# GpSimd makes m and the turn fractions of sub-tiles two to four, and TensorE spreads the three maxima over partitions

## The reference, cut to what matters

```python
# x: (32, 128, 64, 2), real and imaginary part of C; H = 128 states, N = 64, L = 1024
A   = -exp(inv_A_real) + 1j * A_imag;  dtA = A * exp(log_dt)
Cc  = B * C * (exp(dtA) - 1) / A
h   = 2 * einsum('chn,hnl->chl', Cc, exp(dtA * ell)).real       # (32, 128, 1024)
h   = h + layernorm(h) @ attn_w.T + attn_b
y   = layernorm(h)
out = h + y @ W.T + b + sum_e softmax(y @ Wr.T)[e] * 2 * (y @ A[e].T) @ Bm[e].T
```

## Time and profile before

| | |
|---|---|
| median of 3 runs | 817.31 us (816.65 to 817.73) |
| the profiled execution's own time | 814.75 us |
| its span, first to last instruction | 812.9 us, so 1.85 us lie around it |
| PE busy | 776.4 us, 96% |
| DVE busy | 626.1 us, 77% |
| ACT busy | 527.2 us, 65% |
| POOL busy | 6.2 us, 1%, in 21 instructions |
| mean granted TensorE clock | 0.989 of full speed |

### The profile page before, as it was taken

One profiled execution on the slowest core, in us unless ns is written; L12 is line 12 of the kernel. 1 busy time (PEld: TensorE's weight loads), 2 busy tenths in 40 slices (PEclk: granted clock), 3 DMA queues, 4 the chain that ended last, 5 costly groups with the idle time before them and its releaser, 6 DMA issues.

```text
span 812.9 us, 14991 instructions
## 1 busy us (share of the span) xinstructions
PE 776.4 (96%) x5390; PEld 390.0 (48%) x5390; DVE 626.1 (77%) x1250; ACT 527.2 (65%) x884; POOL 6.2 (1%) x21
## 2 busy tenths in 40 slices
PE   3777899999999999999999999999999999999998
PEld 2643344444444444444444444444444444444443
DVE  6799797778777877787778777777887787778522
ACT  5777785767677666757677576667767575765210
POOL 2000000000000000000000000000000000000000
PEclk9989999999999999999999999999999999999999
DMA  8839543435333233334333333433324243423223
GB/s 298 280 72 166 107 98 66 91 59 98 77 76 72 64 85 67 82 77 94 63 73 74 71 83 66 97 77 68 81 55 93 60 89 77 90 52 74 56 52 77
DMA packets 185709, 72.28 MB, mean 89 GB/s; under 512 B 174097, under 2 KB 179089, under 8 KB 185561
## 3 DMA queue, kind: packets, MB, share of 16 engines
q1 hardware_dynamic: 185592, 71.90, 40.2%
q10 hardware_dynamic: 96, 0.13, 0.0%
HBM read 14.06 MB, written 16.78 MB: 38 GB/s over the span
## 4 chain that ended last, share of the span: by engine, by line
PE 88%; DVE 6%; issue 3%; ACT 2%; DMA 0%; SPq 0%; POOL 0%; POOLq 0%; DVEq 0%; ACTq 0%
PE ps_g L549 39%; PE ps_g L489 39%; PE ps_a L480 5%; PE ps_g L560 2%; PE ps_g L681 1%; PE ps_p L537 1%; DVE stage L1287 1%; DVE params L994 1%; PE ps_p L539 1%; DVE wa_lo L1279 0%; PE ps_p L554 0%; ACT decay L728 0%; DVE h_tok L1149 0%; DVE h_tok L1188 0%; DVE result L1287 0%
## 5 line engine op out<-in xcount | busy, mean ns | idle before, releaser
L489 PE MATMUL ps_g<-wa_hi,x 128*128 128x512 f16 x1024 | 270.1, 379 | 2.6 <-DMA x<-x_tok 1.6
L549 PE MATMUL ps_g<-wf_hi,x 128*128 128x512 f16 x992 | 265.2, 380 | 0.6 <-DVE h_tok L1188 0.6
L489 PEld LDWEIGHTS ps_g<-wa_hi,x 128*128 128x128 f16 x1024 | 97.6, 98 | 122.8 <-issue 6.6
L489 PE MATMUL ps_g<-wa_lo,x 128*128 128x512 f16 x512 | 153.6, 379 | 0.0
L549 PE MATMUL ps_g<-wf_lo,x 128*128 128x512 f16 x496 | 149.3, 380 | 0.0
L549 PEld LDWEIGHTS ps_g<-wf_hi,x 128*128 128x128 f16 x992 | 95.0, 98 | 107.5 <-issue 2.2
L1250 DVE SCALAR_TENSOR_TENSOR result<-ps_g,unscale,h_tok 128x1024 f32<-128x1024 f32 x31 | 39.8, 1284 | 84.2 <-PE ps_g L560 84.2
L752 ACT ACTIVATE junk<-ps_a,stat 128x1024 bf16<-128x1024 f32 x32 | 35.6, 1114 | 76.9 <-DVE stat L1152 76.8
L489 PEld LDWEIGHTS ps_g<-wa_lo,x 128*128 128x128 f16 x512 | 50.1, 98 | 60.1
L549 PEld LDWEIGHTS ps_g<-wf_lo,x 128*128 128x128 f16 x496 | 48.5, 98 | 58.5 <-issue 0.5
L758 ACT ACTIVATE junk<-h_tok,stat 128x1024 bf16<-128x1024 f32 x32 | 36.7, 1148 | 59.1 <-DVE stat L1192 59.1
(11 more groups left out here) (208 smaller groups left out, 919.3 us busy)
## 6 DMA issues: line engine op xcount, KB each, us to landing
out<-result SPq DMA_DIRECT2D x124, 128.0 KB, 2.1
stage<-in_L_ffn_W SPq DMA_DIRECT2D x8, 512.0 KB, 13.8
x_raw<-in_x SPq DMA_DIRECT2D x38, 64.0 KB
wf_hi<-in_x SPq DMA_DIRECT2D x1, 2048.0 KB, 9.8
h_tok<-in_L_attn_weight SPq DMA_DIRECT2D x2, 512.0 KB, 3.9
x<-in_L_attn_weight SPq DMA_DIRECT2D x2, 512.0 KB, 6.9
result<-in_L_attn_weight SPq DMA_DIRECT2D x2, 512.0 KB, 8.8
x<-x_tok SPq DMA_TRANSPOSE x64, 3.2
```

The source lines that it names most:

```text
L489: mm = pe.matmul(ps[:, o, :], x1_part(part, ps is ps_g2)[:, k, :], ws[:, k, o * HALF:(o + 1) * HALF], start=k == 0 and part == 0 and ws is ...
L549: pe.matmul(ps_g2[:, o, :], xs[:, k, :], ws[:, k, o * HALF:(o + 1) * HALF], start=k == 0 and xs is x2_hi and ws is wf_hi, stop=False)
```

## The change

`partition_all_reduce` is gone from GpSimd. For each bound TensorE now transposes the column of 128 values into one row of PSUM, DVE takes the maximum of the row, and TensorE multiplies that one value by a row of 128 ones, which puts it on every partition. GpSimd takes over the subtraction of `round_turns` and the three instructions of `make_m` for sub-tiles (0, 1), (1, 0) and (1, 1); from (2, 0) on all stays on DVE. GpSimd's small products for the factor k are written in another order, with `wexp` last, and ACT's wait for it goes from `s_pre_pool` 4 to 10.

```diff
+BY_POOL = (1, 2, 3)
@@ tensor
+            def turn_m_tops():
+                pe.wait_ge(s_x_squares, 1)
+                pe.wait_ge(s_pre_dve, EXPS + 26)
+                for k in range(2):
+                    mm = pe.transpose(ps_a[0:1, 1, k * P:(k + 1) * P], m_top[:, k:k + 1], ident[:, :])
+                mm.then_inc(s_tops_t, 1)
+            def spread_m_top():
+                pe.wait_ge(s_row_top, 2)
+                pe.matmul(spread(ps_a[:, 1, :]), ones_row[:, :], top_row[:, 2:3]).then_inc(s_wall, 1)
+            def turn_weight_tops(k):
+                pe.wait_ge(s_top, k + 1)
+                pe.transpose((ps_x, ps_p)[k][0:1, P:2 * P], top[:, k:k + 1], ident[:, :]).then_inc(s_tops_t, 1)
+            def spread_weight_top(k):
+                pe.wait_ge(s_row_top, k + 3)
+                pe.matmul(spread((ps_x, ps_p)[k][:, :]), ones_row[:, :], top_row[:, 3:4]).then_inc(s_wall, 1)
@@
                 mm.then_inc(s_pre_pe, 1)
+            turn_m_tops()
+            spread_m_top()
             square_attn(5, 8)
@@
             s4(0, 0)
+            turn_weight_tops(0)
             square_ffn(10, 11)
+            spread_weight_top(0)
@@
             turn_weight(4)
-            pe.wait_ge(s_top, 2)
+            turn_weight_tops(1)
+            spread_weight_top(1)
+            pe.wait_ge(s_power, 6)
             turn_weight(5)
@@ gpsimd
+            pool.wait_ge(s_small, 64)
+            (den, k_re, k_im, then after s_pre_dve EXPS: k1, ga, ga, den, k_re, k_im, wexp)
-            (the three partition_all_reduce)
+            def fractions(T, i):
+                pool.wait_ge(s_round, 2 * T + i + 1)
+                pool.tensor_tensor(turn[:, :, :], turn[:, :, :], phase[:, :, :], ALU.subtract).then_inc(s_frac, 1)
+            fractions(0, 1)
+            make_m(0, 1)
+            fractions(1, 0)
+            make_m(1, 0)
+            fractions(1, 1)
+            make_m(1, 1)
@@ vector
+            m_row_top()
             scale_m(0, 3)
@@
             weight_norms(0, ps_g2[:, 0, 0:P])
+            weight_row_top(0)
@@
             weight_norms(1, ps_p[:, 0:P])
+            weight_row_top(1)
             split_scales(1)
             attn_lo(4)
-            make_m(0, 1)
             make_u(0, 1)
```

More of the change, by code:

```diff
@@ L963, in _, with make_m @@
                                steps_a[:, 2:NA].unsqueeze(2).broadcast_to((P, KA, N)), ALU.mult).then_inc(s_pre_pool, 1)
[L964 to L983, removed]
+            def make_m(T, i):
+                J = 2 * T + i
+                pool.wait_ge(s_xt_sb, T + 1)
+                pool.wait_ge(s_s4, J)
+                pool.wait_ge(s_m, J)
+                pool.wait_ge(s_q, 2)
+                for part, dst in enumerate((m, m_im)):
+                    c, f = m_factors(T, i, part)
+                    pool.tensor_tensor(dst[:, :, :].rearrange("p h (a c) -> p h a c", a=KA), c, f, ALU.mult)\
+                        .then_inc(s_terms, 1)
+                pool.wait_ge(s_terms, 2 * J + 2)
+                pool.tensor_tensor(m[:, :, :], m[:, :, :], m_im[:, :, :], ALU.add).then_inc(s_m, 1)
+            def fractions(T, i):
[7 more added lines that the diff above has]
+            make_m(1, 1)
         @block.vector
@@ L1014, in _ @@
[L1014 to L1020, removed]
@@ L1027, in _ @@
[L1027 to L1033, removed]
@@ L1311, in split_lora_b @@
                                   ALU.subtract).then_inc(s_lbn, 1)
+            for tile, value in ((ones[:, :], 1.0), (ones_row[:, :], 1.0), (half_pi[:, :], pi / 2), (quarter[0:N, :], 0.25),
+                                (quarter[N:P, :], 0.0), (eps[:, :], EPS), (steps_a[:, 0:1], 0.5),
+                                (steps_a[:, 1:2], 1.0)):
+                last = dve.memset(tile, value)
+            last.then_inc(s_fill, 1)
+            dve.wait_ge(s_fill, 1)
+            dve.wait_ge(s_small, 64)
@@ new lines, in _ @@
+            link(dve.tensor_scalar, exp_out, exp_in, 1 / factorial(7), None, ALU.mult)
+            for k in range(6, 0, -1):
+                link(dve.scalar_tensor_tensor, out=exp_out, in0=exp_out, scalar=1 / factorial(k), in1=exp_in,
+                                              op0=ALU.add, op1=ALU.mult)
+            link(dve.tensor_scalar, exp_k.bitcast(U32), exp_k, 127.0, 2.0 ** 23, ALU.add, ALU.mult)
+            link(dve.scalar_tensor_tensor, out=exp_out, in0=exp_out, scalar=1.0, in1=exp_k, op0=ALU.add,
+                                          op1=ALU.mult)
@@ new lines, in _ @@
+            assert done[0] == EXPS + 26
+            for dst, part in ((wa, 0), (wb, 1)):
+                tt(dst.rearrange("p s a n -> p (s a) n"), w2.rearrange("p s a n -> p (s a) n"),
+                   g[:, part:part + 1, :].broadcast_to((P, 2 * KA, N)), ALU.mult)
+            tt(qn[:, :, 0:N], wa[:, 0, :, :], wb[:, 1, :, :], ALU.subtract)
+            link(dve.scalar_tensor_tensor, out=qn[:, :, N:2 * N], in0=wa[:, 1, :, :], scalar=-1.0,
+                                          in1=wb[:, 0, :, :], op0=ALU.mult, op1=ALU.subtract)
@@ L1314, in _ @@
+            tt(qn[:, :, 2 * N:3 * N], wb[:, 1, :, :], wa[:, 0, :, :], ALU.subtract)
+            assert done[0] == PRE
+            m_row_top()
             scale_m(0, 3)
@@ L1366, in _ @@
             ffn_lo(15)
-            make_m(1, 0)
             dve.wait_ge(s_wf_0, 32)
```

167 lines of the change are left out of this document (93 added, 74 removed).

## The result

| | before | after |
|---|---|---|
| time, median of 6 runs each on one chip | 817.05 us (814.50 to 818.19) | 821.67 us (820.22 to 825.95) |
| after / before | | 1.0067, 95% interval 1.0047 to 1.0087 |
| profiled execution: time, span | 814.75, 812.9 us | 821.36, 819.5 us |
| start of `s4(1, 1)` in it | 100.36 us | 105.27 us |

The change made the kernel slower. The forecast was 821.7 us with a chance of 0.7 for slower, and both hold. The two profiled executions are 6.6 us apart, more than the 5.5 us of the ratio, and the two medians are 4.6 apart.

A forecast was written before the change was run, and what follows sets the result against it. PE, busy 709.0 of 712.5 us from s4(1, 1) on, was taken as the bound, so prologue delays count. They build to a start 4.4 later: 817.31 + 4.4 = 821.7 us, range 817.4 to 823.6.

The forecast's parts named there:

- The frame: From s4(1, 1) on, instructions are the same and PE is busy, so the end moves by what its start moves.
- The last stretch: Rounding to s4(1, 1): GpSimd's fractions and m alternate with DVE's low_1(1, 0) and make_u(1, 1); start 104.75 instead of 100.36, +4.4.
- The bound of m: Prologue, first step of scale_m: round trip over PE and DVE replaces the all-reduce, +1.4, bounds +0.9 to +1.9.
- The first load of code: GpSimd's affine select at the start: load taken as skipped, nothing won behind block 4's transfer; 0, with 1.4 as bound.
- The bound of the weight: Attention weight's maximum behind s4(0, 0): DVE waits for PE, the scale begins at 33.95, +2.3 on its own.
- What GpSimd costs: GpSimd's large products: 2.4 us for 1024 elements, 1.28 for 512; GpSimd and DVE run one at a time on SBUF inputs.
- From there to x2(0, 0): Second weight scale through project to ffn_part: turn_weight(6) +2.85, normalise_1(0, 1) and project +2.4, ffn_part and s4(1, 0) +1.8.
- the second trip: Round trip over PE and DVE behind weight_norms(1), ahead of the second scale: 1.2 us, both engines waiting for each other.
- Hardly exclude: Rival: DVE and GpSimd hardly exclude each other; 818.7 us, chance 0.20 with the first load skipped, 0.10 with it kept.
- the first load stays: Rival: GpSimd's code load at the start remains, on top of the forecast; +5.8, 823.1 us, chance 0.20.
- Early start carries through: Rival: load skipped, q transpositions 1.5 sooner, both round trips hidden, if together under 1 us; -2.6, 814.7 us, chance 0.10.
- The sum: Whole kernel: +4.4, giving 819.15 us for the profiled execution and 821.7 for the median; chance 0.40 with the load skipped.

The follow-up runs named there:

- e3: Changed kernel with each m made by GpSimd ahead of its sub-tile's turn fractions instead of behind them; 1.0125 of the kernel before.
- e2: Kernel before, all-reduces kept, with m and turn fractions of sub-tiles (1, 0) and (1, 1) made by GpSimd; 1.0033 of the kernel before.
- e6: Changed kernel with m and fractions of sub-tile (1, 1) back on DVE; 1.0041 of the kernel before.
- e7: Kernel before with one unused product added at the end of GpSimd's list, behind its last all-reduce; 0.9998 of the kernel before.
- e9: Kernel before, all-reduces kept, with m and turn fractions of sub-tile (1, 0) alone made by GpSimd; 0.9995 of the kernel before.
- e4: Changed kernel with the attention weight maximum's round trip put ahead of m(0, 0) on DVE and s4(0, 0) on PE; 1.0064 of the kernel before.
- e8: Changed kernel with sub-tile (1, 1)'s m and fractions back on DVE and the weight's round trip ahead of s4(0, 0); 1.0018 of the kernel before.
- e12: Kernel before plus 60 unneeded GpSimd products of 512 numbers beside the steady loop, from the sixth s4 on; single execution's span 838.7 us.
- e5: Changed kernel itself, unchanged, timed again on another chip; 1.0093 of the kernel before.

## Why the prediction was right, step by step

- **The frame** (the end moves by what `s4(1, 1)` moves). It failed by 1.7 of the 6.6 us of the profiled pair: the stretch behind took 714.2 in the four executions where PE had waited 3.3 us for GpSimd's m, and 712.5 to 712.9 in eight where it waited 2.4 or less or the wait was filled; in e3, with 714.66, PE had waited 3.04 and 0.78 us shortly ahead of `s4(1, 1)`, which took 3.64. The prediction named another sign for this, a wait of PE after `s4(1, 1)`; what broke the frame was the clock.
- **The last stretch** was right in mechanism and in size. Forecast 104.75, measured 105.27, or 104.52 without the later block 4. Fractions, low_1(1, 0) and the first product stood in the order forecast, each behind the one before. Then GpSimd's second product (101.90) got ahead of `make_u(1, 1)` (101.97), not the other way round; one behind the other, the sum is the same. Last stretch alone: +2.23 (16.91 less 14.68), forecast 2.6. e2 and e6 show it with and without the cause.
- **The bound of m.** +1.83 on the first step of `scale_m`, or +1.08 without block 4's 0.75, against +1.4, inside its bounds. But the sum hid two larger terms of opposite sign. With the code already loaded and an all-reduce, `s4(0, 0)` comes 8.17 to 8.24 us after block 4 (e2, e7, e9); with the round trip 10.73 to 11.58. The trip costs 2.5 or more, and the load that goes away gives 1.6 back in the profile of before, whose block 4 was the earliest of all.
- **The first load of code** is gone, as taken. That "nothing is won" by it was wrong as a step: 1.6 us are won at `s4(0, 0)`. At the end of the kernel nothing is seen of it (0.9998).
- **The bound of the weight.** The scale came 2.94 us after `s4(0, 0)` began instead of 0.67: +2.27, forecast 2.3. e4 and e8 take 1 to 1.9 us of it back.
- **What GpSimd costs.** 2.36 us for 1024 elements (2.4), 1.07 for 512 in the two products by q (1.28 was taken), and one at a time, shown by e12. The 2.4 was in part luck: the line was drawn through the 0.73 of the earlier trace rows, which DVE had lengthened. In after and in e7 the same product takes 0.62, and the line would have given 1.8. That the tensor-scalar counts too was the rule of the Trainium skill ("SBUF — State Buffer", Who interferes with whom). The 0.37 in the earlier trace rows showed no delay, but that instruction had begun first, at 10.86 against GpSimd's 10.97; `xn`'s 1.62 and the rounding's 1.51 settle it.
- **From there to x2(0, 0).** turn_weight(6) came 3.57 later, 2.82 without block 4, forecast 2.85, the second trip 1.41 (6.03 instead of 4.62 from turn_weight(4) to turn_weight(6); 1.2 was forecast). (The 2.8 in 40.75 + 2.8 was not worked out: 3.7 - 0.63 is 3.07.) Behind it two misses cancelled. `s4(0, 1)` came 4.83 later, since PE's clock was low for longer than in the profile of before, and project 4.73 later, where +2.4 was forecast. But PE had waited only 2.11 us for project instead of 3.64, and went from there to `s4(1, 0)` in 2.49 us at a granted clock of 1.00, where before it had taken 4.54 at 0.62. Of these 2.05 us, 0.63 are the wait for keep_h2 that the prediction took out, the rest is the clock, which was not in the sum. So `s4(1, 0)` is +2.68, or 1.93 without block 4, beside a forecast of +1.8, and that nearness is luck.
- **The rivals.** "Hardly exclude" is out by e12, "the first load stays" by the first row of GpSimd. "Early start carries through" named a true gain and lost, since its condition, round trips under 1 us together, was far off.
- **The sum.** Forecast +4.4, measured 5.5 and 7.6 us on two chips. The 1.65 us of clock in `s4(1, 1)` are the term that was missing at the end. The mechanisms named were right, all but the frame; that the total came so near is also owed to the two misses ahead of `s4(1, 0)`.

Open: how much of the loss ahead of `s4(0, 1)` is PE's clock. In all nine executions with the maxima on TensorE turn_weight(6) took 1.97 us, at half the clock; with an all-reduce it was 1.1 in three executions and 1.97 in two. One execution of each doesn't tell a rule from luck. e7 against before shows that it is worth up to 2.3 us. Open as well: why the first 36 matmuls of attention(0, 1) took 7.8 us in before, e7 and e12 and 9.5 in all other executions.

## What to carry to other kernels

Work moved to GpSimd isn't free because GpSimd was idle: it takes its time from the DVE instructions beside it that read two SBUF operands, and from those like the rounding and `xn`, which read one and take 0.68 and 0.81 us where two operands take 1.22. So move only what stands beside DVE's PSUM reads or DVE's own waits, and keep it out of a chain that ends in a matmul. A round trip of one value over TensorE and DVE costs its hops and whatever stands ahead of each hop in its engine's order. Here an all-reduce of 0.37 us on an idle engine beat it, and where it is replaced, each hop belongs in a wait that both engines have anyway. And a stretch that is "the same instructions" can still change by the clock at which it starts: a wait that went from 2.4 to 3.3 us cost 1.7 us more than itself, and one that went from 3.64 to 2.11 gave back 1.4.

## What the runs showed of the hardware that was not expected

- A product of 8 numbers on DVE took 1.04 us behind a product of GpSimd (e3), and one of 32 numbers 0.91 instead of 0.19 (e12): the delays, 0.87 and 0.72, go by GpSimd's instruction (1.25 us beside the first, 1.07 where nothing blocks it), not by the length of DVE's.
- The code that GpSimd's last instruction needed stays from one execution of a program to the next: the affine select starts at 1.18 to 1.42 us where the program ends with an ordinary operation (after, e7), and at 9.05 where it ends with an all-reduce.
- After a wait of 3.3 us on PE the next 32 matmuls took 3.32 to 3.58 us (after, e2, e4, e5); after waits of 1.8 to 2.4 us at the same place they took 1.93. At another place a wait of 1.63 us was followed by a granted clock of 1.00 in e7 and of 0.82 in e9, so the length of the wait alone does not say what the clock does.
